# Value phase of an attention and routed-memory kernel: replaced slots marked by +3e38, mask and logits in one step, fp32r scores, another order of the steps

## The chip, the cores and the metric

The kernel runs on one core of one Trainium2 chip. The metric is device time in microseconds, a median over runs of the same program. Trainium2's core has five engines that run their own instruction queues in order and meet through semaphores: TensorE (PE in the profile, its weight loads are PEld), VectorE (DVE), ScalarE (ACT), GpSimd (POOL) and SyncE (SP), which here issues the DMAs.

## The reference

`x` has 16 batches of 128 x 1024. First comes a linear attention over `ctx`, with layer norm and a residual, and then a second block on the result. The change lies in the second block:

```python
query = h @ Wq.T                                  # h: layer norm of x, 1024 columns -> 64
rk = aux_keys @ Wr.T                              # 256 slots
router_scores = einsum(query @ Wr.T, rk) / sqrt(48) + log_rel
top_scores, top_idx = top_k(router_scores, 8)     # 8 of 256 slots
attn = einsum(query, aux_keys[top_idx]) / sqrt(64) + log_rel[top_idx]
w = softmax(attn)
aux_out = einsum(w, aux_values[top_idx]) @ Wvd.T @ Wvu.T
u = clip(log1p(var(h)) / mean * 0.5 + sigmoid(gelu(h @ Wu1.T + bu1) @ Wu2.T + bu2) * 2.5, 0, 5)
gate = sigmoid(w1 * clip((u - 0.5) / 1.5, 0, 1) + bias);  gate = where(gate < 0.05, 0, gate)
out = x + (h + gate * aux_out)
```

The kernel doesn't gather. For every row it takes the scores of all 256 slots, masks those outside the eight largest so far down that their exponential is zero, and multiplies the weights of all 256 slots with the value table.

## The kernel before, in words

The work goes in tiles of one batch (128 rows, 1024 columns), 16 tiles, numbered b. Three phases follow each other on the engines and overlap at their ends: the attention (`PERIODS`, to about 540 us), the hidden phase and the value phase. No planner is used: the order on each engine is written out by hand, and each wait is a semaphore with a constant.

**The hidden phase** is `hidden_step(b)`, once on each engine, b from 0 to 16. TensorE transposes the normalised tile b + 1 (L529) into one of two PSUM slots (`slot` is k_slot, q_slot), ScalarE copies it to `hT_hi` in fp32r (L776) and VectorE subtracts to get `hT_lo` (L1113). Then TensorE multiplies tile b with the weights, eight groups of three fp32r products of 320 columns (L542, products(b) below). VectorE adds the bias (L1119), copies the 64 columns of the query to `q_rows` (L1122); ScalarE applies gelu (L780) and later sums (L784). From step 9 on TensorE transposes two queries per step (L549, `queries(b)`: queries 0 and 1 in step 9, 12 and 13 in step 15, 14 and 15 in step 16), and VectorE copies them to `query` (L1126, `query_copy`). In step 13 a sum over the rows (L561) waits for the queries of step 12. Scores 0 and 1 (L555) are made at the end of step 14, behind products(14), scores 2 and 3 behind products(15).

**score(b)** is one fp32 product of the transposed query with `scoreB`, 512 columns: 256 router scores and 256 logits, `log_rel` included through a row of ones. It goes to a PSUM bank, for b from 2 on `gm` or `ob` by turns; score(b) waits until tile b - 2 is through `top_logits`.

**The value phase** is a loop over i. At its start, tile 0 to 3 partly done, TensorE waits until all queries are copied (L687). In period i, in this order:
- TensorE (L690): score(i + 1), z_product(i - 2) (L667, fp32, waits for `wT_copied` and for `z_split` of the tile before), w_transpose(i - 1) (L659), f_product(i - 3) (L681, L682: fp32r, four products of 128x512, waits for `z_split` of its own tile).
- VectorE (L1306): top_replace(i) (L1168, the eight largest become -3e38), z_low(i - 3) (L1194, the lower half of zT by a subtraction, raises `z_split`), top_mask(i) (L1173, 1 where replaced equals the scores), top_max(i + 1) (L1163, waits for score(i + 1)), top_logits(i) (L1179, mask x -3e38 + logits), every second period a reciprocal (L1190), logit_max(i) (L1184). In periods 2 and 3 the gate's steps come in between (L1145 to L1158).
- ScalarE (L899): softmax_exp(i - 1) (L880), in period 1 the last unit_sum and the gate's first tanh, in period 3 its second (L910), f_scale(i - 4) for tiles 0 to 11 (L897), zT_copy(i - 2) (L891), wT_copy(i - 1) (L886).
- GpSimd (L1026): per tile 0 to 11 the addition of x (L1031), every second tile output_scale (L1015).
- Tiles 12 to 15 (`BY_VECTOR` = 4) are scaled and added in one instruction by VectorE, `finish` (L1203), instead of f_scale and GpSimd's addition.
- SP sends each tile out, in order (L414, L420), from four buffers `y_out`.

```python
                pe.wait_ge(z_split, b + 1)                       # f_product(b)
                ...
            for i in range(1, B + 3):                            # TensorE
                if 4 <= i + 1 < B:
                    score(i + 1)
                if has(i - 2):
                    z_product(i - 2, i % 2)
                if has(i - 1):
                    w_transpose(i - 1, (i - 1) % 2)
                if has(i - 3):
                    f_product(i - 3, (i - 3) % 2)
```

## Time and profile before

| | us |
|---|---|
| median of 3 runs | 663.33 (662.93 to 663.96) |
| the profiled execution | 663.27 |
| its span | 661.5 |
| TensorE, VectorE busy in it | 625.1, 579.0 |
| ScalarE, GpSimd busy in it | 419.5, 366.4 |

The span is the time from the first to the last instruction in the trace. Busy times leave out waiting, semaphores and the issue of DMAs. A timeline row has the start, the duration, the engine, the line, the operation, what it writes and reads, and a count; idle time ahead of it and what ended that stand in brackets. Instructions of one engine overlap a little in their rows, as the next one is fed while the last drains, so what a step costs its engine is the distance between two starts. The ends of matmuls are modelled.

### The profile page before, as it was taken

Reading aid. Unit: us, or ns where it says so; the run is one execution under the profiler, and the core shown is the slowest. Engines: PE = TensorE matmul, PEld = TensorE weight load, DVE = VectorE, ACT = ScalarE, POOL = GpSimd, SP = SyncE. Lnnn points to the kernel's source line nnn. Section 1 sums busy time; section 2 is a strip of 40 time slices with the busy share of each in tenths; the row PEclk is TensorE's granted clock in tenths of the full one; section 3 lists DMA queues with packets and bytes.
Section 4 is the critical chain, followed back from the end, with each engine's and each line's share of the span. In section 5 each row is a group of like instructions: output and inputs, shape, how many; then the busy total and the mean of one; then the engine's idle time right before and its main releaser. Section 6 shows DMA issues by size and latency. Waiting matters only on the chain.

```text
span 661.5 us, 11769 instructions
## 1 busy us (share of the span) xinstructions
PE 625.1 (95%) x3974; PEld 546.4 (83%) x3974; DVE 579.0 (88%) x788; ACT 419.5 (63%) x844; POOL 366.4 (55%) x275
## 2 busy tenths in 40 slices
PE   4699999999999999999999999999999799999896
PEld 2487888888888888888888888888889799998574
DVE  4697899999999999999999999999997656866897
ACT  4355676666666666666666766666573856584784
POOL 2434355565655647464646565656546576752294
PEclk9799999999999999999999999999999899999898
DMA  7644244434434343434343434443234100000056
GB/s 262 190 122 121 81 143 112 144 86 143 124 100 133 102 133 102 135 96 136 101 136 104 133 97 134 123 130 97 65 101 148 41 1 2 1 1 1 33 209 268
DMA packets 52779, 72.57 MB, mean 110 GB/s; under 512 B 10112, under 2 KB 43424, under 8 KB 52464
## 3 DMA queue, kind: packets, MB, share of 16 engines
q1 hardware_dynamic: 52336, 70.43, 35.6%
q0 software_dynamic: 384, 1.40, 0.7%
q8 instruction: 32, 0.52, 0.4%
q14 instruction: 27, 0.22, 0.1%
HBM read 29.85 MB, written 8.39 MB: 58 GB/s over the span
## 4 chain that ended last, share of the span: by engine, by line
PE 45%; DVE 29%; issue 19%; ACT 3%; DMA 2%; SPq 2%; POOL 1%; DVEq 0%; ACTq 0%; POOLq 0%
PE gm L468 9%; DVE qm L1075 7%; DVE qsum L1085 7%; PE ob L491 6%; PE gm L542 4%; PE turn L542 4%; DVE nkm L1056 3%; DVE qs_sb L1078 3%; DVE st L1042 3%; DVE st L1100 3%; PE q_slot L428 2%; PE turn L499 2%; DVE kt L1061 2%; PE k_slot L428 2%; PE k_slot L430 2%
## 5 line engine op out<-in xcount | busy, mean ns | idle before, releaser
L942 POOL TENSOR_TENSOR qs_sb<-qs_sb,qrec 128x1024 f32<-128x1024 f32 x64 | 122.0, 1907 | 211.6 <-DVE qrec L1089 211.6
L723 ACT ACTIVATE ek<-k_slot,nkm 128x1024 f32<-128x1024 f32 x62 | 69.1, 1114 | 104.4 <-DVE nkm L1056 104.4
L491 PE MATMUL ob<-mt_sb,q_hd 128*128 128x128 f32 x1024 | 127.3, 278 | 3.7 <-POOL mt_sb L948 3.1
L491 PEld LDWEIGHTS ob<-mt_sb,q_hd 128*128 128x128 f32 x1024 | 122.5, 193 | 8.4 <-issue 3.5
L468 PE MATMUL gm<-ekT,ctxT 128*128 128x256 f32 x512 | 118.2, 379 | 0.0
L468 PEld LDWEIGHTS gm<-ekT,ctxT 128*128 128x128 f32 x512 | 97.0, 190 | 14.8 <-DMA ekT<-kt 0.3
L733 ACT ACTIVATE qs_sb<-qs_sb 128x1024 f32<-128x1024 f32 x64 | 68.5, 1070 | 42.4 <-DVE qs_sb L1078 42.4
L1056 DVE TENSOR_REDUCE nkm<-k_slot 128x1 f32<-128x1024 f32 x62 | 74.2, 1197 | 17.6 <-PE k_slot L430 17.6
L1061 DVE STREAM_TRANSPOSE kt<-ek 128x1024 f32<-128x1024 f32 x64 | 78.6, 1228 | 5.8 <-ACT ek L723 5.8
L1085 DVE TENSOR_REDUCE qsum<-qs_sb 128x16 f32<-128x1024 f32 x64 | 76.9, 1202 | 5.2 <-ACT qs_sb L733 5.2
L1078 DVE TENSOR_TENSOR qs_sb<-q_slot,qm 128x1024 f32<-128x1024 f32 x64 | 78.4, 1225 | 2.2
L1075 DVE TENSOR_REDUCE qm<-q_slot 128x16 f32<-128x1024 f32 x64 | 75.3, 1177 | 0.0
L428 PE MATMUL k_slot<-ctx_hi,WkT_hi 128*128 128x512 f32 x124 | 55.1, 445 | 13.1 <-DVE ctx_lo L1246 7.4
L454 PE MATMUL turn<-ident,qs_sb 128*128 128x128 f32 x512 | 66.3, 273 | 0.0
L454 PEld LDWEIGHTS turn<-ident,qs_sb 128*128 128x128 f32 x512 | 59.6, 141 | 7.8
L738 ACT COPY q_hd<-turn 128x1024 f32<-128x1024 f32 x64 | 64.3, 1005 | 2.0 <-PE turn L454 2.0
L428 PE MATMUL q_slot<-WqT_hi,xn_hi 128*128 128x512 f32 x128 | 55.8, 436 | 6.1 <-DVE qs_sb L1078 5.2
L429 PE MATMUL q_slot<-WqT_hi,xn_lo 128*128 128x512 f32 x128 | 50.6, 396 | 0.0
L430 PE MATMUL q_slot<-WqT_lo,xn_hi 128*128 128x512 f32 x128 | 50.6, 396 | 0.0
L430 PE MATMUL k_slot<-ctx_lo,WkT_hi 128*128 128x512 f32 x124 | 50.1, 404 | 0.0
L429 PE MATMUL k_slot<-ctx_hi,WkT_lo 128*128 128x512 f32 x124 | 49.6, 400 | 0.0
L968 POOL TENSOR_TENSOR x_all<-x_all,hbuf 128x1024 f32<-128x1024 f32 x16 | 38.7, 2428 | 9.8 <-ACT hbuf L770 9.8
(195 smaller groups left out, 1270.7 us busy)
## 6 DMA issues: line engine op xcount, KB each, us to landing
ekT<-kt SPq DMA_DIRECT2D x512, 64.0 KB, 2.0
ctx_in<-ctx_rows SPq DMA_DIRECT2D x16, 512.0 KB, 4.6
x_all<-x SPq DMA_DIRECT2D x16, 512.0 KB, 3.6
ctxT<-ctx_cols SPq DMA_DIRECT2D x16, 512.0 KB, 4.0
out<-q_hd SPq DMA_DIRECT2D x15, 512.0 KB, 2.6
Wuq_in<-Wuq_cols SPq DMA_DIRECT2D x1, 1280.0 KB, 5.4
x_all<-values_cols POOLq DMA_DIRECT2D x1, 1024.0 KB, 6.1
WvuT_in<-WvuT_raw SPq DMA_DIRECT2D x1, 512.0 KB, 4.6
```

The costliest lines, as they stand in the source:

```text
L428: nc.tensor.matmul(dst, lhs[0], rhs[0], start=True, stop=False)
L429: nc.tensor.matmul(dst, lhs[1], rhs[0], start=False, stop=False)
L430: return nc.tensor.matmul(dst, lhs[0], rhs[1], start=False, stop=True)
L454: last = nc.tensor.transpose(turn[:, (2 * t + n) * P:(2 * t + n + 1) * P], qs_sb[:, i % 2, n * HALF + t * P:n * HALF + (t + 1) * P], ident ...
L468: last = nc.tensor.matmul(gm[:, cols], ctxT[:, b % 2, j, :], ekT[:, 2 * half:2 * half + 2, :, j * BLK:(j + 1) * BLK], start=(j == 0), stop ...
L491: last = nc.tensor.matmul(ob[:, (j % 4) * C:(j % 4 + 1) * C], q_hd[:, t, j * P:(j + 1) * P], mt_sb[:, b % 2, t, :], start=(t == 0), stop=( ...
L942: nc.gpsimd.tensor_tensor(e, e, qrec[:, i % 2, :].unsqueeze(2).broadcast_to([P, PAIR, DH]), ALU.mult).then_inc(q_mul, 1)
L1056: V.tensor_reduce(nkm[:, i:i + 1], k_psum(b, i)[:, :], AX, ALU.max, negate=True).then_inc(k_max, 1)
L1061: V.transpose(kt[:, i, :], ek[:, i % 2, :]).then_inc(k_T, 1)
L1075: V.tensor_reduce(qm[:, :], q, AX, ALU.max).then_inc(q_max, 1)
L1078: V.tensor_tensor(qs_sb[:, i % 2, :].rearrange("p (m d) -> p m d", d=DH), q, qm[:, :].unsqueeze(2).broadcast_to([P, PAIR, DH]), ALU.subtra ...
L1085: V.tensor_reduce(qsum[:, :], qs_sb[:, i % 2, :].rearrange("p (m d) -> p m d", d=DH), AX, ALU.add).then_inc(q_sum, 1)
```

## The change

- `top_replace` writes +3e38 (`FAR`) in place of the eight largest scores. `top_logits` computes replaced - 3e38 + logits in one instruction: the chosen slots keep their logits, the others fall to about -3e38. `top_mask`, its tile and its semaphore go.
- Scores are three fp32r products (hi x hi, lo x hi, hi x lo). For that each query is split in `query_split` (a copy to fp32r, then a subtraction), and `scoreB` once in `score_halves`, in step 10. The halves take the place of tiles that are no longer needed.
- Scores 0 and 1 move from behind products(14) to ahead of them; VectorE works on tiles 0 to 3 earlier in steps 14 to 16. TensorE's wait for all queries moves to f_product(1).
- VectorE's gate steps and ScalarE's second tanh move up by about a period.
- TensorE's order in a period becomes score, f, z, w. VectorE's becomes replace, max, logits, z_low, logit_max, reciprocal, finish. ScalarE's f_scale and copies keep their order.
- Tiles 4 and 8 are now finished by VectorE as well, beside 12 to 15; `own(b)` counts the tiles of the same kind up to b, for the semaphores.

```diff
-BY_VECTOR = 4
+BY_VECTOR = (4, 8, 12, 13, 14, 15)
-NEG = -3.0e38
+FAR = 3.0e38
...
+        def own(b):
+
+            return sum((n in BY_VECTOR) == (b in BY_VECTOR) for n in range(b + 1))
...
             def score(b):
                 pe.wait_ge(query_done, b + 1)
+                pe.wait_ge(score_split, 2)
+                if b < 2:
+                    pe.wait_ge(hT_hi_done, B - 1)
+                    pe.wait_ge(hT_lo_done, B - 1)
                 if b >= 4:
                     pe.wait_ge(masked, b - 1)
-                nc.tensor.matmul(score_psum(b), query[:, b, :], scoreB[:, :], start=True, stop=True).then_inc(scores, 1)
+                product(score_psum(b), [query_hi[:, b, :], query_lo[:, b, :]],
+                        [score_hi[:, :], score_lo[:, :]]).then_inc(scores, 1)
...
+                    if b == B - 2:
+                        for n in range(2):
+                            score(n)
                     if b < B - 1:
                         hidden_products(b, b % 2)
...
-                if b - 2 < B - BY_VECTOR:
-                    wait(pe, f_scaled, b - 1)
-                else:
-                    pe.wait_ge(y_last, b - 2 - (B - BY_VECTOR) + 1)
+                if b == 1:
+                    pe.wait_ge(query_done, B)
+                if b >= 2:
+                    pe.wait_ge(y_last if b - 2 in BY_VECTOR else f_scaled, own(b - 2))
...
-            pe.wait_ge(query_done, B)
             pe.wait_ge(wvu_hi, 1)
             pe.wait_ge(wvu_lo, 1)
             for i in range(1, B + 3):
                 if 4 <= i + 1 < B:
                     score(i + 1)
+                if has(i - 3):
+                    f_product(i - 3, (i - 3) % 2)
                 if has(i - 2):
                     z_product(i - 2, i % 2)
                 if has(i - 1):
                     w_transpose(i - 1, (i - 1) % 2)
-                if has(i - 3):
-                    f_product(i - 3, (i - 3) % 2)
...
+                if has(i - 4) and i - 4 not in BY_VECTOR:
+                    f_scale(i - 4, i % 2)
+                if has(i - 2):
+                    zT_copy(i - 2, i % 2)
+                if i == 2:
                     act.wait_ge(gate_arg, 1)
                     nc.scalar.activation(gb[:, :], ga[:, :], ACT.Tanh, bias=half3[:, 2:3],
                                          scale=half3[:, 1:2]).then_inc(gate_tanh, 1)
-                if 0 <= i - 4 < B - BY_VECTOR:
-                    f_scale(i - 4, i % 2)
-                if has(i - 2):
-                    zT_copy(i - 2, i % 2)
...
+            for b in range(B):
+                if b % 2 == 0 and b + 2 < B:
                     output_scale(b + 2)
-                pool.wait_ge(f_scaled, b + 1)
-                pool.wait_ge(y_done, b + 1)
-                nc.gpsimd.tensor_tensor(y_out[:, b % YB, :], y_out[:, b % YB, :], X[:, b, :],
-                                        ALU.add).then_inc(y_ready, 1)
-            output_scale(B - 2)
+                if b not in BY_VECTOR:
+                    pool.wait_ge(f_scaled, own(b))
+                    pool.wait_ge(y_done, b + 1)
+                    nc.gpsimd.tensor_tensor(y_out[:, b % YB, :], y_out[:, b % YB, :], X[:, b, :],
+                                            ALU.add).then_inc(y_ready, 1)
...
-            def query_copy(b, k):
-                dve.wait_ge(rows_T, b + 1)
-                V.tensor_copy(query[:, b, :], query_psum(b)).then_inc(query_done, 1)
+            def query_split(b):
+                for n in b:
+                    dve.wait_ge(rows_T, n + 1)
+                    V.tensor_copy(query_hi[:, n, :], query_psum(n)).then_inc(query_hi_done, 1)
+                for n in b:
+                    dve.wait_ge(query_hi_done, n + 1)
+                    V.tensor_tensor(query_lo[:, n, :], query_psum(n), query_hi[:, n, :].bitcast(F32),
+                                    ALU.subtract).then_inc(query_done, 1)
+
+            def score_halves():
+                dve.wait_ge(score_ready, 2)
+                dve.wait_ge(log_rel_in, 16 * 2)
+                V.tensor_copy(score_hi[:, :], scoreB[:, :]).then_inc(score_split, 1)
+                dve.wait_ge(score_split, 1)
+                V.tensor_tensor(score_lo[:, :], scoreB[:, :], score_hi[:, :].bitcast(F32),
+                                ALU.subtract).then_inc(score_split, 1)
...
-                wait(dve, outside_done, b)
-                V.match_replace(replaced[:, :], top8[:, b % 2, :], score_psum(b)[:, 0:NSLOT], NEG).then_inc(top_step, 1)
-
-            def top_mask(b):
+                wait(dve, masked, b)
+                V.match_replace(replaced[:, :], top8[:, b % 2, :], score_psum(b)[:, 0:NSLOT], FAR).then_inc(top_step, 1)
+
+            def top_logits(b):
+
                 dve.wait_ge(top_step, 2 * b + 2)
-                wait(dve, masked, b)
-                V.tensor_tensor(outside[:, :], replaced[:, :], score_psum(b)[:, 0:NSLOT],
-                                ALU.is_equal).then_inc(outside_done, 1)
-
-            def top_logits(b):
-                dve.wait_ge(outside_done, b + 1)
                 wait(dve, w_done, b - 1)
-                V.scalar_tensor_tensor(logits[:, b % 2, :], outside[:, :], NEG, score_psum(b)[:, NSLOT:2 * NSLOT],
-                                       ALU.mult, ALU.add).then_inc(masked, 1)
+                V.scalar_tensor_tensor(logits[:, b % 2, :], replaced[:, :], FAR, score_psum(b)[:, NSLOT:2 * NSLOT],
+                                       ALU.subtract, ALU.add).then_inc(masked, 1)
...
-                    top_max(0)
-                    top_replace(0)
-                    for n in queries(b):
-                        query_copy(n, n % 2)
-                    top_mask(0)
-                    top_max(1)
-                    top_logits(0)
-                if b == B:
                     top_replace(1)
-                    top_mask(1)
+                    query_split(queries(b))
                     top_logits(1)
                 if has(b - 1):
                     unit_weights(b - 1, (b - 1) % 2)
+                if b == B - 2:
+                    top_max(0)
+                    top_replace(0)
+                    top_max(1)
+                    top_logits(0)
+                    logit_max(0)
                 if b == B - 1:
-                    logit_max(0)
-                if b == B:
                     logit_max(1)
-                    top_max(2)
                 if b < B:
                     unit_bias(b, b % 2)
                     query_rows(b)
                 if EARLY < b < B - 1:
-                    for n in queries(b):
-                        query_copy(n, n % 2)
+                    query_split(queries(b))
+                if b == EARLY + 2:
+                    score_halves()
+                if b == B:
+                    top_max(2)
+                    top_replace(2)
+                    top_max(3)
+                    top_logits(2)
+                    logit_max(2)
 
             def weights_low(weights, raw, done):
                 dve.wait_ge(done, 1)
@@ -1303,29 +1324,29 @@
                 if b == EARLY + 5:
                     log_mean()
                 hidden_step(b)
-            for i in range(2, B + 3):
+            gate_argument()
+            top_replace(3)
+            z_low(0, 0)
+            top_logits(3)
+            gate_value()
+            logit_max(3)
+            weight_reciprocal(0)
+            query_split(queries(B))
+            top_max(4)
+            for i in range(4, B + 3):
                 if i < B:
                     top_replace(i)
-                if i == 2:
-                    for n in queries(B):
-                        query_copy(n, n % 2)
-                if has(i - 3):
-                    z_low(i - 3, (i - 3) % 2)
-                if i < B:
-                    top_mask(i)
                 if i + 1 < B:
                     top_max(i + 1)
                 if i < B:
                     top_logits(i)
+                if has(i - 3):
+                    z_low(i - 3, (i - 3) % 2)
+                if i < B:
+                    logit_max(i)
                 if i % 2 == 0 and i <= B:
                     weight_reciprocal(i - 2)
-                if i < B:
-                    logit_max(i)
-                if i == 2:
-                    gate_argument()
-                if i == 3:
-                    gate_value()
-                if B - BY_VECTOR <= i - 4:
+                if i - 4 in BY_VECTOR:
                     finish(i - 4, i % 2)
             finish(B - 1, (B - 1) % 2)
 
```

## Rows read from the trace of the kernel before

**Rows 1.** The page, part 1: engine, busy us (share of the span), instructions

```profile
PE 625.1 (95%) x3974; PEld 546.4 (83%) x3974; DVE 579.0 (88%) x788; ACT 419.5 (63%) x844; POOL 366.4 (55%) x275
```

**Rows 2.** Windows of the trace: stretch, length, busy of each engine, clock, DMA

```profile
core 0: us, PE busy (x) PEld busy (x) DVE busy (x) ACT busy (x) POOL busy (x), PEclk, DMA share, GB/s
624.00:648.00 24.00, 24.00 (x119) 17.53 (x118) 22.54 (x75) 21.60 (x50) 23.84 (x14) 1.00 0.50 198
```

**Rows 3.** The chain of waits in order of time: start us, us, what

```profile
624.36 0.86 PE gm L555 x2
...
646.42 0.87 PE ob L555 x2
```

**Rows 4.** Timeline of TensorE: start us, us, engine, line, operation, out<-in, count

```profile
623.18 0.48 PE L681 MATMUL q_slot<-WvuT_hi,zT 128*128 128x512 f32 x1
...
650.05 0.47 PE L681 MATMUL k_slot<-WvuT_hi,zT 128*128 128x512 f32 x1
```

**Rows 5.** Timeline of VectorE, one period of the loop

```profile
631.79 0.29 DVE L1194 TENSOR_TENSOR zT<-turn,zT 64x128 fp32r<-64x128 f32 x1
632.12 0.42 DVE L1173 TENSOR_TENSOR outside<-replaced,gm 128x256 f32<-128x256 f32 x1
632.61 0.43 DVE L1163 MAX8 top<-ob 128x8 f32<-128x256 f32 x1
632.96 0.40 DVE L1179 SCALAR_TENSOR_TENSOR logits<-outside,gm 128x256 f32<-128x256 f32 x1
633.28 0.16 DVE L1190 RECIPROCAL wrec<-wsum 128x2 f32<-128x2 f32 x1
```

**Rows 6.** Timeline of TensorE, the same period

```profile
629.95 0.61 PE L667 MATMUL turn<-wT,VV 128*128 128x128 f32 x4
...
630.53 0.48 PE L681 MATMUL k_slot<-WvuT_hi,zT 128*128 128x512 f32 x1
630.85 0.39 PE L682 MATMUL k_slot<-WvuT_lo,zT 128*128 128x512 f32 x1
...
631.55 1.02 PE L555 MATMUL ob<-scoreB,query 128*128 128x512 f32 x2
```

**Rows 7.** Timelines of VectorE and TensorE, the last z_low and f(15)

```profile
654.43 0.29 DVE L1194 TENSOR_TENSOR zT<-turn,zT 64x128 fp32r<-64x128 f32 x1
...
654.78 0.50 PE L681 MATMUL q_slot<-WvuT_hi,zT 128*128 128x512 f32 x1
655.12 0.40 PE L682 MATMUL q_slot<-WvuT_lo,zT 128*128 128x512 f32 x1
```

**Rows 8.** Timeline of VectorE, a finish of a whole tile

```profile
653.12 1.28 DVE L1203 SCALAR_TENSOR_TENSOR q_hd<-q_slot,oscale,x_all 128x1024 f32<-128x1024 f32 x1
```

**Rows 9.** Timelines of VectorE and TensorE, steps 11 to 15 of the hidden phase

```profile
588.65 1.23 DVE L1113 TENSOR_TENSOR hT_lo<-k_slot,hT_hi 128x1024 fp32r<-128x1024 f32 x1 [1.19 <-ACT hT_hi L776]
...
596.84 0.35 PE L561 MATMUL gm<-logsum,ones 128*128 128x1 f32 x2 [0.92 <-DVE query L1126]
...
606.31 1.88 PE L555 MATMUL k_slot<-scoreB,query 128*128 128x512 f32 x4
608.03 0.27 PE L549 MATMUL gm<-ident,q_rows 128*128 128x128 f32 x1
...
606.77 0.28 DVE L1126 COPY query<-gm 128x128 f32<-128x128 f32 x1
```

**Rows 10.** Timelines of ScalarE and TensorE, the start of the value phase

```profile
614.16 0.51 ACT L880 ACTIVATE w_sb<-logits,nlmax 128x256 f32<-128x256 f32 x1
...
615.97 0.41 PE L659 MATMUL turn<-ident,w_sb 128*128 128x128 f32 x2 [2.10 <-issue]
```

**Rows 11.** Windows of the trace, two stretches with TensorE's granted clock

```profile
16.40:19.80 3.40, 2.28 (x18) 1.78 (x20) 2.35 (x2) 1.92 (x4) 1.41 (x1) 1.00 0.00 0
...
617.30:620.70 3.40, 3.40 (x13) 2.32 (x13) 2.91 (x12) 1.42 (x5) 0.00 (x0) 0.52 0.00 0
```

**Rows 12.** Timeline of ScalarE, one copy of zT

```profile
650.11 0.27 ACT L891 CAST zT<-turn 128x128 fp32r<-128x128 f32 x1
```

39 lines of the change are left out of this document (18 added, 21 removed).

## The prediction

> **What bounds the kernel now.** I began with the busy time on the page: TensorE has work for 95% of the span [rows 1]. That is an average over stages, so I looked only at the stage that the diff touches, from 590 us to the end. The windows give it: from 624 to 648 us TensorE is busy for all of 24.00 us, GpSimd for 23.84, VectorE for 22.54 and ScalarE for 21.60, at the full clock, 2.4 GHz [rows 2]. Four engines are nearly level. The chain of waits tells which of them ends last: it stays on TensorE and comes by a score every time round, at 624.36 and nine tiles later at 646.42 [rows 3]. So one tile costs 22.06 / 9 = 2.45 us, and f(1), the value product of tile 1, starts at 623.18 [rows 4].
>
> The reader should see one more thing in VectorE's timeline [rows 5]: in a period **z_low (L1194) runs ahead of mask (L1173) and max (L1163)**. The max waits for this period's scores. z_low, for which TensorE waits before its next z and f products, is ahead of that wait. So within a period nothing runs from the scores through VectorE back to TensorE.
>
> **The steady loop after the change.** I write i for the period. TensorE's new order is score(i+1), f(i-3), z(i-2), transpose w(i-1). VectorE's is replace(i), max(i+1), logits(i), z_low(i-3), logit_max(i). Both queues run in order. f(i-3) waits for `z_split`, which z_low(i-3) raises; z_low(i-3) now stands behind max(i+1), which waits for score(i+1); and score(i+2) stands on TensorE behind f(i-3), z(i-2) and w(i-1). That closes a ring with one turn per tile. Everything TensorE still has to do in the period is queued behind the wait of f. The length of a turn:
> - score as three fp32r products of 128x512: L681 and L682 are such products. They start 0.32 us (the first behind fp32 work) and 0.23 us apart and one lasts 0.40 [rows 6]: 0.32 + 0.23 + 0.40 = 0.95 to the end of the third;
> - end of score to max: the scores of 631.55 last 1.02, max starts at 632.61 [rows 6, 5]: 0.04;
> - max to logits 0.35, logits to the instruction behind it 0.32 (632.61, 632.96, 633.28) [rows 5]. The new logits step is one instruction of L1179's kind, operands and size, so it is priced by that row; it depends only on an old replace;
> - z_low 0.29 [rows 5];
> - z_low to f: 654.43 + 0.29 = 654.72, f starts at 654.78: 0.06; its four products take 0.34 + 3 x 0.23 = 1.03 after such a wait [rows 7];
> - z and w: 630.53 less 629.95 = 0.58 [rows 6].
>
> The sum is 0.95 + 0.04 + 0.35 + 0.32 + 0.29 + 0.06 + 1.03 + 0.58 = **3.62 us** against 2.45. It holds from f(1) (i = 4) to f(11) (i = 14): ten turns, 36.2 us for 24.5, so +11.7. The link from z_low to f is read once and may be 0.1 longer; the first fp32r score may lose the 0.09 that the change of type costs. A turn lies between 3.5 and 3.7.
>
> **What is removed, and why it returns nothing.** The mask goes, 0.42 us of VectorE per tile [rows 5]. VectorE works 22.54 of 24.00 us now, 2.30 per tile [rows 2]; without the mask 1.88 of a turn of 3.62, and the rest is its wait for scores, which the 0.42 only lengthens. The finishes of tiles 4 and 8 move to VectorE, 1.28 each [rows 8]: 1.88 + 1.28 = 3.16 still fits in a turn; if it did not, each would cost up to 1.3. Score falls from 0.86 [rows 3] to 3 x 0.23 = 0.70 of TensorE's time; that is inside the 3.62. The Trainium skill, FP8 and Floating Point Precision, TensorE Precision Notes, says that true FP32 takes four passes; by that one fp32r product is 0.86 / 4 = 0.21, and a turn would be 0.06 shorter. ScalarE and GpSimd lose two tiles each and get more than 1 us of slack per turn. SP sends the outputs in order as before, each behind its tile, and none is ready ahead of an earlier one for long; the stores are further apart.
>
> **The lead-in**, in order of time:
> - VectorE now splits each query (two copies, then two subtractions of 128x128, about 0.20 us apart like the two copies of now) and once splits scoreB (128x512) in step 10. There it idles 1.19 us before a subtraction of 128x1024 that takes 1.23 [rows 9]; two instructions of half its columns cost at most that, the query split 0.40, and the next who needs VectorE is half a step off. So steps 9 to 12 don't move. In step 13 TensorE waits for the last query copy of step 12 (0.92 idle before L561) [rows 9]: +0.40.
> - Scores 0 and 1 move ahead of products(14) and cost 6 x 0.23 = 1.39 there. So far they filled the gap between products(14) and the transposes of queries 12 and 13 (606.31 to 608.03) [rows 9]. The last of these (608.03 + 0.11) waits for the split of query 11, which begins where the copy does, 606.77, and needs 0.60 + 0.28 and 0.15 to TensorE: 1.49 behind 606.31 instead of 1.83. Together 1.39 - 0.34 = +1.05, with the step before +1.45.
> - exp(0) stands on ScalarE behind gelu(15) and a table load (it starts at 614.16) [rows 10], so it moves with products(15) to 615.6, however early its logits are. w(0), held until 615.97 by the last query copies, is free 0.15 after exp(0) and its read, 616.4: only +0.4.
> - Then, by the durations above, VectorE does logits(2) 616.3, the gate argument to 617.7, replace(3), z_low(0) 618.4, logits(3), the gate value, logit_max(3), a reciprocal, four query instructions, max(4) 620.6, replace(4), max(5) 621.6, logits(4), z_low(1) 622.3: f(1) starts at 622.6 if TensorE's clock stays full. Now the clock falls here: after 2.10 us without work before 615.97 [rows 10] it is 0.52 from 617.30 to 620.70 [rows 11]. In the new order the same stretch is thin again; at half rate score(4), f(0), z(1) and score(5) end later and f(1) is at 623.7.
>
> I take **623.1**, between the two, since nothing tells them apart. Before, it was 623.18, so the lead-in as a whole gives nothing.
>
> **The tail.** After score(15) the ring opens, but f(i-3) now stands ahead of z(i-2), so the z_low of each tile follows its z product with nothing between: f 1.03, z 0.61 [rows 6], to ScalarE 0.04, zT copy 0.27 [rows 12], 0.04, z_low 0.29, 0.06 = 2.34 per tile. Before, f(12) to f(15) took 654.78 - 650.05 = 4.73 [rows 4, 7]; now 3 x 2.34 = 7.0. f(11) to f(12) is 2.3 as well. Behind f(15) stands what stood there before, finish(14), finish(15) and the last stores, 661.50 - 654.78 = 6.72; with the stores less crowded I take 6.4.
>
> **The sum.** 623.1 + 36.2 + 4 x 2.34 + 6.4 = 675.1 us of span. The profiled run took 663.27 for a span of 661.5, so 1.8 lie around it: 676.9, as a round number **677.0**. The median of the runs, 663.33, lies 0.06 from the profiled one. A measurement of this kernel can tell about 0.2% (1.3 us) from no change.
>
> **The rivals.**
> - *The ring doesn't close*: z_low(i-3) gets through VectorE before score(i+1) ends, or TensorE is a score ahead; that is the point from which it decides. TensorE would then pay 2.45 - 0.16 = 2.29 per tile: 622.6 + 11 x 2.29 + 11.45 (650.05 to the end) = 659.2, in time **661.0**, 0.35% faster; with the tail as above, 663.3, no change. Against it: z_low comes after max(i+1) in every period from i = 4, and score(i+1) after w(i-2), so only an index that I misread would open the ring. Chance 0.04 for faster, 0.03 for no change.
> - *TensorE's clock falls again and again.* A turn leaves TensorE about 1.2 us without work. A fall lasted 3.4 us (617.30 to 620.70) [rows 11]; with TensorE at work for some 75% of it and half of that lost, each costs 1.3, and five of them in 36 us make 683.5. For it: the fall at 617. Against it: from 16.40 to 19.80 us TensorE worked 2.28 of 3.40 us and the clock stayed at 1.00 [rows 11], which is close to the 2.4 of 3.6 of a turn. Chance 0.08. The Trainium skill, TensorE: Matmul & The Clock Gate, "A second HAM failure mode: psum-queue depth-cycling", says that short idle times between groups of matmuls can make the clock swing between its levels; that speaks for this rival, and the row of 16.40 is the nearest that this trace has, against it.
> - *My forecast*: chance 0.85, its own range 672 to 681.5.
>
> The range: the turn gives -1.2 or +0.8; the clock in the lead-in 0.5 either way; the tail 1.0 either way (VectorE's finishes lie in it); the link of 0.1, the stores and the finishes of tiles 4 and 8, if not covered, up to 2.6. Summed on the side where they agree, that is 672 to 681.5, which leaves out the first rival and nearly all of the second, 0.15. Chances: faster 0.04, same 0.03, slower 0.93.
>
> **What the next profile would show.** Right: TensorE's scores 3.5 to 3.7 us apart in the loop, with 1.1 to 1.3 us idle ahead of the first product of each f, put down to VectorE's zT; VectorE idle some 1.5 us before each max, put down to the scores; GpSimd idle over 1 us a tile; a chain of waits that goes score, max, logits, zT, f, z, w. exp(0) near 615.6 and f(1) between 622.6 and 623.7 would bear out the lead-in, an f every 2.3 to 2.4 us from f(11) on the tail. Wrong: scores 2.3 us apart, an idle time that is put down to another engine, or a clock of 0.50 in several stretches of the loop.

## The result, and the profile after

| | before | after |
|---|---|---|
| median of 4 runs, same chip | 663.64 (662.93 to 664.72) | 677.93 (677.18 to 680.39) |
| ratio | | 1.022, 95% interval 1.019 to 1.0251 |
| profiled execution, its span | 663.27, 661.5 | 677.44, 675.6 |

The kernel became 2.2% slower: 677.9 us, where 677.0 was predicted. I read the views of after in the same order as those of before.

First the windows from 624 to 648 us (length; busy time and instructions of PE, PEld, DVE, ACT, POOL; granted clock, DMA share, GB/s):

```profile
624.00:648.00 24.00, 16.97 (x90) 12.74 (x88) 13.11 (x41) 12.19 (x32) 14.06 (x10) 1.00 0.33 132
```

Before, TensorE worked for all 24.00 us of this stretch and GpSimd for 23.84 [rows 2]. Now no engine is busy for more than 71% of it. Nothing is short of capacity, so what sets the pace has to be a chain of waits. The chain that ended last names it (start, duration, what the time went to; one period):

```profile
630.78 0.50 PE q_slot L693
...
631.98 0.44 PE turn L679 x4
632.42 0.22 PE turn L671 x2
632.64 0.23 PE gm L436
632.87 0.23 PE gm L437
633.10 0.25 PE gm L438
633.35 0.02 issue
633.38 0.04 DVE top L1187
633.41 0.31 issue
633.73 0.40 DVE logits L1198
634.13 0.03 issue
634.16 0.30 DVE zT L1213
634.47 0.04 issue
634.51 0.50 PE k_slot L693
```

Read it as a circle: f, z, w transpose and score on TensorE, then max, logits and z_low on VectorE, and the next f waits for that z_low. Before, the chain stayed on TensorE [rows 3]. From 630.78 to 634.51 one turn takes 3.73 us; before, a tile took 2.45.

The same turn in VectorE's timeline (start, duration, line, operation, output <- input, idle time ahead and what ended it):

```profile
633.38 0.43 DVE L1187 MAX8 top<-gm 128x8 f32<-128x256 f32 x1 [1.66 <-PE gm L438]
633.73 0.40 DVE L1198 SCALAR_TENSOR_TENSOR logits<-replaced,ob 128x256 f32<-128x256 f32 x1
634.16 0.29 DVE L1213 TENSOR_TENSOR zT<-turn,zT 64x128 fp32r<-64x128 f32 x1
634.49 0.42 DVE L1203 TENSOR_REDUCE nlmax<-logits 128x1 f32<-128x256 f32 x1
```

and the first product of an f in TensorE's timeline, for f(1), f(4), f(11), f(12) and f(15):

```profile
623.34 0.50 PE L693 MATMUL q_slot<-WvuT_hi,zT 128*128 128x512 f32 x1 [1.23 <-DVE zT L1213]
...
634.51 0.50 PE L693 MATMUL k_slot<-WvuT_hi,zT 128*128 128x512 f32 x1 [1.17 <-DVE zT L1213]
...
660.58 0.50 PE L693 MATMUL q_slot<-WvuT_hi,zT 128*128 128x512 f32 x1 [1.17 <-DVE zT L1213]
...
662.91 0.50 PE L693 MATMUL k_slot<-WvuT_hi,zT 128*128 128x512 f32 x1 [0.47 <-DVE zT L1213]
...
669.86 0.50 PE L693 MATMUL q_slot<-WvuT_hi,zT 128*128 128x512 f32 x1 [0.69 <-DVE zT L1213]
```

Each engine waits for the other once in every turn: VectorE 1.66 us for the scores, TensorE 1.17 us for z_low. Ten turns from f(1) to f(11) take 660.58 - 623.34 = 37.24 us, **3.72 each**. The tail tiles take (669.86 - 660.58) / 4 = 2.32 each. What stands behind f(15) takes 675.6 - 669.86 = 5.74.

Against the trace of before, f(1) comes 0.16 us later, f(1) to f(11) takes 12.7 longer (24.52 there), f(11) to f(15) 2.2 longer (7.08 there), and what stands behind f(15) is 1.0 shorter (6.72 there). That makes the 14.1 us of span. Nine tenths of the loss lie in the loop.

### The profile page after: what moved, and what is told of

Same layout as the page of the kernel before. It is cut to its first block, busy times and chain, and to the rows that moved or that the text cites. A ratio compares the mean times of both kernels' runs of the same rounds, so it can differ in the third digit from the quotient of the medians.

```text
span 675.6 us, 11791 instructions
## 1 busy us (share of the span) xinstructions
PE 624.3 (92%) x3990; PEld 547.7 (81%) x3990; DVE 581.9 (86%) x792; ACT 416.0 (62%) x842; POOL 362.0 (54%) x273
## 4 chain that ended last, share of the span: by engine, by line
PE 42%; DVE 31%; issue 19%; ACT 3%; DMA 2%; SPq 2%; POOL 1%; DVEq 0%; ACTq 0%; POOLq 0%
PE gm L476 9%; DVE qm L1086 7%; DVE qsum L1096 7%; PE ob L499 6%; PE gm L550 4%; DVE nkm L1067 3%; DVE qs_sb L1089 3%; PE turn L550 3%; DVE st L1053 3%; DVE st L1111 2%; PE q_slot L436 2%; PE turn L507 2%; DVE kt L1072 2%; PE k_slot L436 2%; PE k_slot L438 2%
```

## The experiments

### Where z_low stands

The theory: of everything in the diff, the place of z_low behind max costs the time. The rivals: TensorE's new order costs it, or the two additional finishes on VectorE do. **z_low ahead of max, nothing else undone:**

```diff
                     top_replace(i)
+                if has(i - 3):
+                    z_low(i - 3, (i - 3) % 2)
                 if i + 1 < B:
                     top_max(i + 1)
                 if i < B:
                     top_logits(i)
-                if has(i - 3):
-                    z_low(i - 3, (i - 3) % 2)
```

> The changed kernel with one step of VectorE put back: z_low(i-3) ahead of max(i+1) in the loop, all else as changed. Theory of the ring (score, max, logits, z_low, f, z, w, score; 3.72 us per turn): with z_low ahead of the wait for scores the ring opens. What is left is TensorE's own 2.3 us per tile and the short ring f, z, zT copy, z_low, f of 2.34 us, the one the tail shows. f(1) near 622.7, ten turns of 2.37, four of 2.34, 5.8 behind f(15), 1.8 around the span: about 663.5 us. Rival (the slowdown comes from the split scores, the finishes on VectorE or the moved gate steps): the time stays above 670 us.

Measured: 666.06 us, ratio to before 1.0028 (1.0016 to 1.004). That returns 11.9 of the 14.3 us. An f comes every 2.38 us, except at two places. VectorE's timeline at one of them, and TensorE's:

```profile
633.45 1.27 DVE L1222 SCALAR_TENSOR_TENSOR q_hd<-k_slot,oscale,x_all 128x1024 f32<-128x1024 f32 x1
...
635.14 0.29 DVE L1213 TENSOR_TENSOR zT<-turn,zT 64x128 fp32r<-64x128 f32 x1
635.47 0.43 DVE L1187 MAX8 top<-gm 128x8 f32<-128x256 f32 x1
635.93 0.42 DVE L1198 SCALAR_TENSOR_TENSOR logits<-replaced,ob 128x256 f32<-128x256 f32 x1
```

```profile
635.49 0.50 PE L693 MATMUL k_slot<-WvuT_hi,zT 128*128 128x512 f32 x1 [1.07 <-DVE zT L1213]
```

The finish of tile 4 (1.27 us) now stands ahead of a z_low for which TensorE waits 1.07 us. f(5) to f(6) takes 635.49 - 631.92 = 3.57 us, and the finish of tile 8 does the same between f(9) and f(10). In the long turn of the changed kernel both finishes lay inside VectorE's wait for the scores; with the ring gone, this cover is gone too. This is what the expectation missed.

**The same with tiles 4 and 8 given back to ScalarE and GpSimd:**

```diff
-BY_VECTOR = (4, 8, 12, 13, 14, 15)
+BY_VECTOR = (12, 13, 14, 15)
```

> The kernel of e1 (z_low ahead of max) with tiles 4 and 8 back on ScalarE and GpSimd. In e1's trace TensorE stands idle 1.07 and 1.11 us before f(6) and f(10), put down to z_low, right behind VectorE's finishes of tiles 4 and 8. Theory: with the ring open a turn is 2.4 us and no longer covers a finish of 1.28 beside VectorE's other 1.9 us; without them both idle times go: 666.1 less 2.2, about 663.9 us. Rival (GpSimd's two more additions cost as much): about 666.

Measured: 663.15 us, 1.0002 (0.9988 to 1.0015), and f(1) to f(11) takes 645.75 - 621.97 = 23.78, 2.38 per tile without exception. So the two finishes cost 1.2 us each by the rows (3.57 less 2.38) once they are uncovered, and nothing in the changed kernel. The medians differ by 2.9; the kernel before, measured beside each of the two, differs by 0.3 as well (663.88 and 663.54). This kernel still has everything else of the diff, and it is as fast as the kernel before: only z_low's place, and the finishes once it is put back, cost time on balance.

**z_low ahead of max, and TensorE's old order (score, z, w, f):**

```diff
                     score(i + 1)
-                if has(i - 3):
-                    f_product(i - 3, (i - 3) % 2)
                 if has(i - 2):
                     z_product(i - 2, i % 2)
                 if has(i - 1):
                     w_transpose(i - 1, (i - 1) % 2)
+                if has(i - 3):
+                    f_product(i - 3, (i - 3) % 2)
```

> The changed kernel with both orders put back: z_low ahead of max on VectorE, and score, z, w, f on TensorE. What remains of the change: mask merged, fp32r scores, gate steps up, tiles 4 and 8 finished by VectorE. Theory: TensorE's 2.3 us per tile bounds the loop, the tail goes back to 4.7 us for three tiles: f(1) 623.3, eleven times 2.30, 11.45 to the end, 1.8: about 661.8 us, 0.3% faster than before. Rival (another engine takes over at 2.45 us): about 663.5 us.

Measured: 665.75 us, 1.0031 (1.0019 to 1.0044), the same as with the new order. The uncovered finishes are there as well, this time ahead of z: TensorE idles 1.21 us before the z at 636.54. TensorE's order isn't what costs the time on balance. In the tail it does cost: f(12) to f(15) takes 4.69 us here, as before (4.73), and 7.01 with the new order. How the kernel with the new order makes up for that, these two traces don't show cleanly, since TensorE's clock fell to 0.50 in the lead-in of this one (620 to 622 us) and stayed at 1.00 in the other.

The expectation, 661.8, missed by 3.9. The finishes are 2.4 of it. The rest is in every second turn: those take 2.55 us for 2.28 (628.61 to 631.16 and 626.33 to 628.61), because z_low comes at 630.06 there, behind the reciprocal and replace, and z begins 0.42 behind the third product of the scores (630.08 to 630.50) instead of 0.23 (627.80 to 628.03) and takes 0.08 longer. The kernel with z_low first of all, further down, doesn't have this.

**z_low between max and logits**, to test whether the ring is as long as what it is made of:

```diff
                     top_max(i + 1)
-                if i < B:
-                    top_logits(i)
                 if has(i - 3):
                     z_low(i - 3, (i - 3) % 2)
+                if i < B:
+                    top_logits(i)
```

> The changed kernel with z_low(i-3) between max(i+1) and logits(i): still behind the wait for scores, but one instruction earlier. Theory of the ring: the turn loses just the way from logits to z_low, 0.43 us, so 3.72 becomes 3.29 us, ten turns give 4.3 us, about 673.6 us. Rival (it is VectorE's amount of work that counts, or a clock, not the order): no change, 677.9 us.

Measured: 674.17 us, 1.0149 (1.0129 to 1.017), with a turn of (656.98 - 626.32) / 9 = 3.41. Taking logits out of the ring shortens it by 3.72 - 3.41 = 0.31: from max to z_low it was 0.35 + 0.43, and it is 0.46 now. The expectation took off the whole 0.43; that it is 0.46 from max, and not 0.35, is what the section on the mis-sized link follows up.

**Only z_low moved, in the kernel before.** Mask, fp32 scores, TensorE's order and the finishes stay:

```diff
-                if has(i - 3):
-                    z_low(i - 3, (i - 3) % 2)
                 if i < B:
                     top_mask(i)
                 if i + 1 < B:
                     top_max(i + 1)
                 if i < B:
                     top_logits(i)
+                if has(i - 3):
+                    z_low(i - 3, (i - 3) % 2)
```

> The kernel before with nothing changed but VectorE's order: z_low(i-3) behind max(i+1) and logits(i). Theory of the ring: fp32 scores 1.02, 0.04 to max, 0.35 to logits, 0.43 to z_low, 0.29, 0.14 to z, 0.44, w 0.14, f 1.01 and the next score: 3.84 us per turn instead of 2.45, eleven turns, +15.3 and some 0.5 in the tail: about 679 us. Rival (the ring needs the new order on TensorE as well): about 664 us.

Measured: 680.35 us, 1.0245 (1.0218 to 1.0273). TensorE's timeline (the z products) and VectorE's:

```profile
629.76 0.68 PE L667 MATMUL turn<-wT,VV 128*128 128x128 f32 x4 [1.26 <-DVE zT L1194]
630.27 0.38 PE L659 MATMUL turn<-ident,w_sb 128*128 128x128 f32 x2
...
633.71 0.68 PE L667 MATMUL turn<-wT,VV 128*128 128x128 f32 x4 [1.26 <-DVE zT L1194]
```

```profile
632.83 0.40 DVE L1179 SCALAR_TENSOR_TENSOR logits<-outside,gm 128x256 f32<-128x256 f32 x1
633.26 0.30 DVE L1194 TENSOR_TENSOR zT<-turn,zT 64x128 fp32r<-64x128 f32 x1
```

One move, without anything else of the diff, costs the kernel before more than the whole change does. The turn is 3.95 us, longer than the 3.72 of the change, because the fp32 score is the longer one. It is 0.11 above the 3.84 that was expected, but this time not by the link to z_low: logits to z_low is 0.43 (632.83 to 633.26), as the expectation had it. The z products, which now begin behind a wait, take 0.51 to the transpose (629.76 to 630.27) where I had counted 0.44; z_low to z is 0.02 longer, and the terms as I wrote them add up to 3.86 and not 3.84.

### The mis-sized link

In three kernels z_low begins 0.11 us later behind its predecessor than another instruction does: 0.43 for 0.32 behind logits (the change, and the kernel before with z_low moved), 0.46 for 0.35 behind max (635.73 to 636.19, with z_low in the middle). And the one behind z_low starts 0.33 later (634.16 to 634.49), when z_low, which lasts 0.29, has ended. z_low overlaps neither neighbour. One thing sets it apart: it is the only instruction of the loop that works on rows 64 to 127. The rival: it is its output type or its in-place form, or simply the wait. **z_low on rows 0 to 63, at the same place** (the subtraction that rows 64 to 127 need is left out):

```diff
-                V.tensor_tensor(zT[VB:P, k, :], z_psum[VB:P, :], zT[VB:P, k, :].bitcast(F32),
+                V.tensor_tensor(zT[0:VB, k, :], z_psum[0:VB, :], zT[0:VB, k, :].bitcast(F32),
```

> The changed kernel with z_low's operands on rows 0 to 63 in place of rows 64 to 127, at the same place in VectorE's order; the subtraction is thereby done on the rows where it isn't needed, and the split of z isn't the reference's (that part of the computation is changed). Theory (the start in another half of the rows keeps z_low from overlapping the instruction before it): logits to z_low 0.32 us in place of 0.43, the next instruction some 0.2 us after z_low's start in place of 0.33, f's starts 3.61 us apart in place of 3.72, ten turns -1.1 us, time about 676.8 us. Rival (it is the type of the output, the in-place form, or the order itself): 0.43 stays, f's starts 3.72 apart, time 677.9.

Measured: 676.02 us, 1.018 (1.0153 to 1.0207). VectorE's timeline and TensorE's next f:

```profile
634.19 0.40 DVE L1198 SCALAR_TENSOR_TENSOR logits<-replaced,ob 128x256 f32<-128x256 f32 x1
634.51 0.28 DVE L1213 TENSOR_TENSOR zT<-turn,zT 64x128 fp32r<-64x128 f32 x1
634.71 0.40 DVE L1203 TENSOR_REDUCE nlmax<-logits 128x1 f32<-128x256 f32 x1
```

```profile
634.84 0.50 PE L693 MATMUL k_slot<-WvuT_hi,zT 128*128 128x512 f32 x1 [1.04 <-DVE zT L1213]
```

Logits to z_low is 0.32, z_low to the next 0.20, TensorE's idle time 1.04 for 1.17, and ten turns take 659.98 - 624.07 = 35.91, **3.59 each**: 1.33 us less. Same type, same form, same waits; only the rows differ. The rival is out. Of the 0.13 per turn 0.11 lies ahead of z_low, and 0.02 between the starts of z_low and f (0.33 for 0.35). The median fell by 1.9 us; 1.3 of it are the ten turns, and the rest is within the spread of the runs (675.46 to 676.68 here, 677.18 to 680.39 there).

The Trainium skill, VectorE: DVE Perf Modes, "Two Vector instructions with no wait between them", states that an instruction whose inputs or output begin in another group of 32 partitions than the last ones did is held until all earlier ones on VectorE have finished. The rows agree, for z_low and for the one that follows it. The page counts SBUF and PSUM apart, by the last instruction that read from each; the kernel with z_low ahead of max shows that too. There max, which reads only PSUM, stands behind z_low, and logits, the next that reads SBUF, starts 0.46 behind max (635.47 to 635.93) for the 0.35 of the changed kernel. The page gives no duration; here it is 0.11 us ahead of z_low and 0.13 behind it.

### The parts that were to save time

**The mask alone**, in the kernel before:

```diff
-                V.match_replace(replaced[:, :], top8[:, b % 2, :], score_psum(b)[:, 0:NSLOT], NEG).then_inc(top_step, 1)
+                V.match_replace(replaced[:, :], top8[:, b % 2, :], score_psum(b)[:, 0:NSLOT], FAR).then_inc(top_step, 1)
...
-                V.scalar_tensor_tensor(logits[:, b % 2, :], outside[:, :], NEG, score_psum(b)[:, NSLOT:2 * NSLOT],
-                                       ALU.mult, ALU.add).then_inc(masked, 1)
+                V.scalar_tensor_tensor(logits[:, b % 2, :], replaced[:, :], FAR, score_psum(b)[:, NSLOT:2 * NSLOT],
+                                       ALU.subtract, ALU.add).then_inc(masked, 1)
```

> The kernel before with the mask merged into the logits step and nothing else. Theory: VectorE's 0.42 us per tile are not on the chain, which stays on TensorE at 2.45 us per tile; no change, 663.7 us, at most 0.5 us less from the steps of tiles 0 and 1. Rival (VectorE, busy 22.54 of 24 us, sets part of the pace): up to 16 x 0.1 less, about 662.

Measured: 663.95 us, 1.0007 (0.9997 to 1.0017). Its window:

```profile
624.00:648.00 24.00, 24.00 (x119) 16.65 (x117) 19.03 (x63) 20.94 (x48) 23.52 (x14) 1.00 0.49 193
```

VectorE falls from 22.54 to 19.03 us, TensorE stays at 24.00. The 3.5 us that VectorE gains turn into waiting.

**The fp32r scores alone**, in the kernel before, with the query split and the split of scoreB that they need:

```diff
-                nc.tensor.matmul(score_psum(b), query[:, b, :], scoreB[:, :], start=True, stop=True).then_inc(scores, 1)
+                pe.wait_ge(score_split, 2)
+                product(score_psum(b), [query_hi[:, b, :], query_lo[:, b, :]],
+                        [score_hi[:, :], score_lo[:, :]]).then_inc(scores, 1)
```

> The kernel before with fp32r scores alone (query split, split of scoreB in step 10), mask, orders and finishes as before. Theory: TensorE's share of a tile falls from 2.45 to 2.29 us, but VectorE (2.30 with the mask, and its wait for scores) and GpSimd (2.43 to 2.45 per addition, twelve in a row) are as long as the old pace, and step 13 waits about 1 us longer: no gain, 663.5 to 665 us. Rival (scores were the whole bound): 0.16 x 11 less, about 662.

Measured: 664.76 us, 1.001 (0.9997 to 1.0024). TensorE does get faster: f(1) to f(10) takes 644.65 - 623.80 = 20.85, 2.32 per tile for 2.45. But GpSimd needs 2.42 for each of its twelve additions (two of them and an output_scale stand from 643.81 to 648.64), and its last ends at 653.35, when TensorE is at f(14). The end, in VectorE's timeline:

```profile
656.12 1.41 DVE L1225 SCALAR_TENSOR_TENSOR q_hd<-q_slot,oscale,x_all 128x512 f32<-128x512 f32 x2 [0.65 <-DMA out<-q_hd]
```

The last finish waits for a store of an earlier tile, since the four output buffers come free in order. Before, this finish waited for nothing.

### Whether the change holds a gain at all

**Everything that saves, without what costs**: merged mask, fp32r scores, TensorE's old order, finishes 12 to 15, z_low first in VectorE's period, scoreB's halves one step later:

```diff
-BY_VECTOR = (4, 8, 12, 13, 14, 15)
+BY_VECTOR = (12, 13, 14, 15)
...
-                if b == EARLY + 2:
+                if b == EARLY + 3:
                     score_halves()
...
             for i in range(4, B + 3):
+                if has(i - 3):
+                    z_low(i - 3, (i - 3) % 2)
                 if i < B:
                     top_replace(i)
...
-                if has(i - 3):
-                    z_low(i - 3, (i - 3) % 2)
                 if i < B:
                     logit_max(i)
```

> Mask merged, fp32r scores and gate steps as changed, but z_low first of all in VectorE's period, score, z, w, f on TensorE, tiles 4 and 8 back to ScalarE and GpSimd, the split of scoreB in step 11. Theory: no ring through the scores, no finish in the loop, TensorE's 2.30 us per tile bounds it: f(1) 622.7, f(12) 25.3 later, 11.45 to the end, 1.8: about 661.2 us. Rival (GpSimd at 2.45 us per tile sets the pace again): about 663.0 us.

Measured: 662.66 us, 0.9993 (0.9981 to 1.0005): no difference from before. The loop is as fast as hoped (f(1) to f(11) 22.80, 2.28 per tile), and the gain goes at the end:

```profile
653.16 1.28 DVE L1222 SCALAR_TENSOR_TENSOR q_hd<-k_slot,oscale,x_all 128x1024 f32<-128x1024 f32 x1 [0.68 <-DMA out<-q_hd]
655.50 1.41 DVE L1222 SCALAR_TENSOR_TENSOR q_hd<-q_slot,oscale,x_all 128x512 f32<-128x512 f32 x2 [1.06 <-DMA out<-q_hd]
```

GpSimd's additions end at 652.7, and finish(14) and finish(15) wait 0.68 and 1.06 us for a buffer. **One tile less for GpSimd, and its output_scale behind its addition:**

```diff
-BY_VECTOR = (12, 13, 14, 15)
+BY_VECTOR = (11, 12, 13, 14, 15)
...
             for b in range(B):
-                if b % 2 == 0 and b + 2 < B:
-                    output_scale(b + 2)
                 if b not in BY_VECTOR:
...
+                if b % 2 == 0 and b + 2 < B:
+                    output_scale(b + 2)
```

> The kernel of e6 with tile 11 finished by VectorE too (five finishes at the end) and GpSimd's output_scale(b+2) behind the addition of tile b. In e6 the finishes of tiles 14 and 15 stand 0.68 and 1.06 us for a store of the tile four before, which GpSimd's twelfth addition (to 652.7) delivers late. Theory: GpSimd ends one addition and 1.2 us earlier, these two waits go, and the end is 1.2 us earlier than in e6: about 661.5 us. Rival (the end is bound by VectorE's finishes or the stores themselves): no change against e6, 662.7.

Measured: 661.48 us, 0.9969 (0.9956 to 0.9982), 0.3% faster than the kernel before. The same two finishes:

```profile
652.54 1.28 DVE L1222 SCALAR_TENSOR_TENSOR q_hd<-k_slot,oscale,x_all 128x1024 f32<-128x1024 f32 x1
653.85 1.41 DVE L1222 SCALAR_TENSOR_TENSOR q_hd<-q_slot,oscale,x_all 128x512 f32<-128x512 f32 x2
```

Both waits are gone; which of the two edits did it, or whether both were needed, isn't shown. The finish of tile 11 has its price too: it starts at 647.23, ahead of a z_low, and TensorE idles 1.16 us before the z at 648.97, so that f(12) to f(13) takes 2.99 us for 1.93 in the kernel ahead of it. That is the price of an uncovered finish once more.

**And scores 0 and 1 back behind products(14)** (VectorE's steps of tiles 0 and 1 move to step 15 with them, not shown):

```diff
-                    if b == B - 2:
-                        for n in range(2):
-                            score(n)
                     if b < B - 1:
                         hidden_products(b, b % 2)
...
                         query_transpose(n, n % 2)
+                if b == B - 2:
+                    for n in range(2):
+                        score(n)
```

> The kernel of e10 with scores 0 and 1 back behind products(14), and VectorE's steps of tiles 0 and 1 in step 15. Theory: in the changed order TensorE waits 1.11 us for the split of query 11 before products(15) because the scores that filled this gap were moved away; back in their place they cover it: f(1) and the end 1.1 us earlier than in e10, about 660.4 us, 0.5% faster than before. Rival (VectorE has too much to do in step 15 and gives it back before exp(0)): as e10.

Measured: 660.86 us, 0.995 (0.9934 to 0.9967). The wait of 1.11 us before the transposes of queries 12 and 13 is gone, and f(1) stands 31.03 us behind unit_weights(10) (591.52 to 622.55) for 32.41 in the kernel ahead of it (589.38 to 621.79), at the full clock in both. This is the fastest version, 0.5% below the kernel before; from the one ahead of it (0.9956 to 0.9982) these runs don't tell it apart.

### The lead-in

**scoreB's halves one step later**, in the changed kernel; one run:

```diff
-                if b == EARLY + 2:
+                if b == EARLY + 3:
                     score_halves()
```

> The changed kernel with the split of scoreB moved from step 10 to step 11. In the changed kernel's trace the split pushed unit_weights of step 10 into an addition of GpSimd, it took 2.63 us instead of 0.42, all of VectorE's steps after it came later and TensorE's wait in step 13 grew from 0.92 to 1.90 us where I had priced 0.40. Theory: in step 11 nothing is pushed into GpSimd's addition, no unit_weights over 0.5 us, the wait in step 13 falls to about 1.3 us, and f(1) comes 0.6 us earlier. About 677.3 us, too little to tell by time; the trace decides. Rival (the query split alone makes the wait): it stays at 1.9.

In step 13 TensorE waited 1.90 us in the changed kernel, and 1.31 with this edit. Its time, 680.77 us, says nothing: in that execution the attention ended some 2.5 us later, and TensorE's clock fell at 620 us. The rows that explain the wait, in VectorE's timeline of the changed kernel:

```profile
587.87 0.61 DVE L1147 CAST score_hi<-scoreB 128x512 fp32r<-128x512 f32 x1
588.52 0.69 DVE L1149 TENSOR_TENSOR score_lo<-scoreB,score_hi 128x512 fp32r<-128x512 f32 x1
589.12 1.22 DVE L1124 TENSOR_TENSOR hT_lo<-k_slot,hT_hi 128x1024 fp32r<-128x1024 f32 x1
590.26 2.63 DVE L1154 TENSOR_TENSOR units<-units,Wu 128x256 f32<-128x256 f32 x1
```

in GpSimd's and TensorE's:

```profile
590.24 2.37 POOL L979 TENSOR_TENSOR x_all<-x_all,hbuf 128x1024 f32<-128x1024 f32 x1 [2.04 <-ACT hbuf L781]
...
597.92 0.35 PE L574 MATMUL gm<-logsum,ones 128*128 128x1 f32 x2 [1.90 <-DVE query_lo L1141]
```

unit_weights(10), an instruction with two inputs in SBUF, takes 2.63 us where it took 0.42 before, and it ends 0.28 behind GpSimd's addition (592.89 and 592.61). The halves pushed it from 589.79 to 590.26 (0.1 of that lies ahead of them), onto the start of that addition. The trace of before has the same thing in earlier steps, in VectorE's timeline and GpSimd's:

```profile
577.08 1.83 DVE L1130 TENSOR_TENSOR units<-units,Wu 128x256 f32<-128x256 f32 x1
...
576.23 2.40 POOL L968 TENSOR_TENSOR x_all<-x_all,hbuf 128x1024 f32<-128x1024 f32 x1 [0.70 <-ACT hbuf L770]
```

There unit_weights starts inside an addition and ends 0.28 behind it (578.91 and 578.63), and at 570.73 it lasts 2.54. So the trace of before already held this price.

The edit takes the collision away, but other kernels show that the halves in step 10 are not enough to cause it. With them in step 10 the two starts stand within 0.03 us of each other in every trace, and it falls one way or the other:

| halves in step 10 | unit_weights(10) | GpSimd's addition | wait in step 13 |
|---|---|---|---|
| the changed kernel | 590.26, 2.63 | 590.24, 2.37 | 1.90 |
| z_low on rows 0 to 63 | 591.21, 2.63 | 591.18, 2.37 | 1.90 |
| z_low ahead of max | 590.61, 0.41 | 590.61, 2.67 | 1.31 |
| the same, TensorE's old order | 590.55, 0.42 | 590.54, 2.67 | 1.31 |
| the same, four finishes | 590.13, 0.41 | 590.13, 2.67 | 1.31 |
| z_low in the middle | 590.75, 0.42 | 590.75, 2.67 | 1.31 |
| fp32r scores alone | 590.47, 0.41 | 590.46, 2.68 | 1.31 |

(start and duration, us; before: 0.92 of wait.) Where GpSimd starts 0.02 us or more ahead, VectorE's instruction is drawn out to 0.28 behind the end of the addition; where they start within 0.01, VectorE's runs at its own pace and GpSimd's addition takes 0.28 longer. So in these rows the wait of step 13 is 0.39 above that of before as a rule, and 0.98 when the collision goes against VectorE.

## Why the prediction was right

**The ring.** All of its path is in the chain of after: the same seven links, in the order in which the prediction put them. Moving one of them out (z_low ahead of max) returned 11.9 us, and putting only that one into the kernel before made it 2.45% slower, some 16 us. The first rival, that it doesn't close, is out. Its point of decision is the order in VectorE's queue, as said.

**The length of a turn** was 3.72 for 3.62, just outside the 3.5 to 3.7 that I gave it. The mis-sized term is "logits to the instruction behind it 0.32". I read it from a pair in which a reciprocal follows; now z_low stands behind logits, and ahead of z_low it is 0.43. The trace of before had a sign of it: z_low lasts 0.29 and the mask starts 0.33 behind its start [rows 5], while each other pair there overlaps by 0.08, save mask and max, where max waits for the scores. Ten turns made it 1.1 us. All other terms held: score 0.94 (632.40 to 633.34), score to max 0.04, max to logits 0.35, z_low to its end 0.29, the link 0.06, f 1.04, z and w 0.58.

**What was to return nothing.** The mask alone gave 3.5 us of VectorE's time and none of the kernel's, as argued. The finishes of tiles 4 and 8 are hidden: no f of the changed kernel waits longer than 1.17 where they stand. The price I gave for their losing that cover, up to 1.3 each, was measured at 1.2.

**The lead-in.** f(1) came at 623.34 for 623.1, but by another way than the sum's. Step 13 took +0.98 in wait for +0.40, which the prediction had ruled out ("steps 9 to 12 don't move"): the split of scoreB moved VectorE's next steps, onto the start of GpSimd's addition. Five other kernels, in which the collision went the other way, had 0.39. The 1.39 for scores 0 and 1 held: they took 1.49 (603.57 to 605.06), and products(14) behind them 0.10 less than before. The last of the transposes of queries 12 and 13 held too: it started 1.48 behind the place where the scores had stood (608.78 to 610.26), for 1.49. But products(15) began 0.25 behind it (610.51) where it had been 0.03, and the sum has no term for that. exp(0) was at 616.49 for 615.6: 0.9 late, of which 0.58 is the collision, 0.2 this start, and 0.1 was there before step 10 (unit_weights(9) at 585.45 for 585.34). In return the clock stayed full from 613.5 to 623.5 us, the end of the range at which I put f(1) at 622.6; 622.6 and the 0.9 make 623.5. So the hit on f(1) is in part luck: two errors of opposite sign.

**The clock** in the loop was 1.00, so the second rival is out: idle times of 1.17 us in every 3.72 didn't bring it down. Whether it falls in the lead-in differs from trace to trace. In the four with the lead-in of before (the kernel before, z_low late in it, the mask alone, the scores alone) it fell to 0.50 each time; in the ten with the changed lead-in, or that lead-in with the halves or the scores moved, it fell in two. One of them is the run with the halves in step 11; in its windows, the columns as above:

```profile
618.00:620.00 2.00, 0.41 (x2) 0.20 (x2) 1.62 (x6) 1.96 (x8) 0.00 (x0) 1.00 0.00 0
620.00:622.00 2.00, 1.95 (x8) 1.86 (x9) 1.36 (x8) 1.21 (x5) 0.00 (x0) 0.53 0.00 0
622.00:624.00 2.00, 2.00 (x7) 1.59 (x6) 1.97 (x10) 0.61 (x3) 0.20 (x1) 0.62 0.00 0
```

After a thin stretch TensorE stands near 1.2 GHz for some 3 us there, at nearly the same work for which the changed kernel was granted 2.4 GHz. What decides between them stays open, and with one trace for each kernel these rows can't tell a kernel's doing from an execution's; to take f(1) between the two cases was as much as the rows allowed.

**The tail** took 2.32 per tile for 2.34. Behind f(15) it was 5.74 for 6.4, the other miss. I had kept most of what stood there before. finish(15) ends 2.70 behind the start of f(15) in after (671.15 + 1.41 less 669.86) and 2.75 before (656.13 + 1.40 less 654.78), so the finishes are the same; what got shorter is the last store, 3.04 us from there to the end of the span for 3.97. The DMA view of the last 9 us has it in its issues (count, KB, median us to landing). After:

```profile
out<-q_hd SPq DMA_DIRECT2D x4, 512.0 KB, 2.9
out<-q_hd SPq DMA_DIRECT2D x2, 256.0 KB, 2.5
```

and before:

```profile
out<-q_hd SPq DMA_DIRECT2D x4, 512.0 KB, 3.5
out<-q_hd SPq DMA_DIRECT2D x2, 256.0 KB, 3.4
```

The last two stores, half a tile each, land 0.9 us sooner, and the ones ahead of them 0.6. I had named this effect ("the stores less crowded") and given it 0.3. No run moves the stores alone, but the other traces fit it: behind f(15) the five further kernels with TensorE's new order, whose tail has an f every 2.3 us, need 5.66 to 5.88. Those with the old order need 6.32 to 8.56, save the two with five finishes in a row (5.74 and 5.79), where f(12) and f(13) stand 2.99 apart.

**The sum**: f(1) +0.24, the ring +1.04, the tail -0.08, the end -0.66, together +0.54 against the 675.1 of span.

**The range** was wider than its terms. On the side of less they give 1.2 + 0.5 + 1.0 below 677.0, which is 674.3; the 672 that I wrote comes out only with the 2.6 of the link, the stores and the finishes taken off as well, though uncovered finishes can only add. The result lies inside either.

## What to carry to other kernels

Before two steps change places in an in-order queue, write down for each what it waits for and who waits for it. If one is waited for by another engine and the other waits for that same engine, the swap can close a ring, and its length is the sum of the links, whatever the busy times say. What lies hidden in such a ring (here two finishes and a merged mask) must be priced again once the ring is opened.

## What the runs showed of the hardware

- Behind or ahead of a VectorE instruction that begins in another part of the rows there is no overlap: 0.43 for 0.32, 0.46 for 0.35, and 0.33 for 0.20 to the next. With the rows as the only difference the first and the last went (0.32 and 0.20); behind max that wasn't tried.
- A 128x256 VectorE instruction with two SBUF inputs took 2.63 us for 0.42 beside an addition of GpSimd that had started 0.02 us before it, and the addition 2.67 for 2.39 where they started level. The held instruction ends 0.28 us behind the addition, in the trace of before too (1.83 and 2.54 us at 577.08 and 570.73). A start that differs by hundredths of a us decides on 0.6 us of TensorE's wait in step 13 (1.90 for 1.31). The Trainium skill, GPSIMD Engine Reference, Specifications, says that the two engines contend for the SBUF interfaces when VectorE reads two inputs there; the rows agree, and put a size to it.
- What fp32r scores save TensorE depends on what stands ahead of them. Behind f, also fp32r, the three take 0.69 us (630.45 to 631.14, the kernel with all orders) for the 0.86 of the fp32 product, and the tile fell from 2.45 to 2.28. Behind the fp32 w transpose, in the order of the change, the first alone takes 0.31 (632.40 to 632.71).
